# Queries projected ahead of the scores in the first attention rounds, a quarter-size zero buffer, and the delta rule's epsilon scaled by the query's norm

## What is computed

```python
h = layernorm(x) * (1 + ca) + sa
x = x + ga * L0_attn(h)        # layer 0: softmax attention, 16 heads of 8, with a position bias
h = layernorm(x) * (1 + cb) + sb
x = x + gb * L0_ffn(h)         # 8 experts, top 1, capacity 640 each
...
x = x + ga * L1_attn(h)        # layer 1: gated delta rule, 16 value heads, 8 key heads of 64
x = x + gb * L1_ffn(h)         # 16 experts that each pick 512 tokens, and a shared one
```

```python
proj = einsum('bld,ed->ble', x, w_in)          # k, v, q
logits = einsum('bhld,bhmd->bhlm', q, k) * scale + bias
out = einsum('bhlm,bhmd->bhld', softmax(logits), v)
```

```python
q = q * rsqrt(sum(q * q) + EPS) * DK ** (-0.5)
o = ...                                        # linear in q
o = o * rsqrt(mean(o * o) + EPS) * norm_w * silu(z)
```

## Time and profile before

| | |
|---|---|
| median of 3 runs | 2565.08 us (2564.73 to 2572.67) |
| profiled execution | 2562.15 us |
| its span, first to last instruction | 2560.4 us |
| busy: PE, PEld, DVE | 2086.0, 1296.3, 1848.1 us |
| busy: ACT, POOL | 1478.8, 788.8 us |
| granted TensorE clock, mean | 0.896 |
| whole program's DMA | 85.57 MB |

### The profile page before, as it was taken

How to read it: one execution, slowest core, us unless ns; L and a number is a source line. 1 busy time by engine, 2 the same in 40 slices (tenths; PEclk the granted TensorE clock), 3 DMA queues, 4 the chain that set the end, 5 groups by cost and what they waited for, 6 DMA issues and landing times. The chain is left out here.

```text
span 2560.4 us, 64355 instructions
## 1 busy us (share of the span) xinstructions
PE 2086.0 (81%) x25432; PEld 1296.3 (51%) x25432; DVE 1848.1 (72%) x4475; ACT 1478.8 (58%) x4032; POOL 788.8 (31%) x851
## 2 busy tenths in 40 slices
PE   6988988988887585488888888888888884778984
PEld 2444444444444363256655555666555563555552
DVE  6777777777776335799999999899999953673333
ACT  3666766766666124357777777777777663222221
POOL 1000100100100243134444444444444431105884
PEclk7999999999998797689999999999999985788997
DMA  6000000000000431100000000000000003334334
GB/s 231 1 1 5 9 5 5 9 5 5 9 5 5 123 97 41 29 11 13 13 13 13 13 13 13 13 13 13 13 13 5 5 4 104 83 100 105 44 44 89
DMA packets 109980, 85.57 MB, mean 33 GB/s; under 512 B 22430, under 2 KB 97858, under 8 KB 109424
## 3 DMA queue, kind: packets, MB, share of 16 engines
q1 hardware_dynamic: 96112, 68.31, 9.1%
q0 software_dynamic: 13568, 13.14, 3.2%
HBM read 59.22 MB, written 22.71 MB: 32 GB/s over the span
## 5 line engine op out<-in xcount | busy, mean ns | idle before, releaser
L565 ACT ACTIVATE Pr<-Pr,nmax 128x512 f32<-128x512 f32 x512 | 341.2, 715 | 190.2 <-DVE nmax L475 187.7
L706 PE MATMUL bank<-ident,Pr 128*128 128x128 f32 x2048 | 305.6, 292 | 83.1 <-DVE PT L484 62.8
L706 PEld LDWEIGHTS bank<-ident,Pr 128*128 128x128 f32 x2048 | 234.9, 148 | 255.2 <-DVE PT L484 160.5
L475 DVE CUSTOM_DVE_ANT_0 Pr<-bank,Tb 128x512 f32<-128x512 f32 x512 | 330.9, 684 | 29.5 <-PE bank L692 28.8
L484 DVE COPY PT<-bank 128x512 f32<-128x512 f32 x256 | 176.6, 690 | 186.5 <-PE bank L720 182.9
L2469 PE MATMUL bank<-Wcv,hw 128*128 128x512 f32 x512 | 245.8, 624 | 4.9 <-ACT bank L2260 3.4
L2073 DVE TENSOR_TENSOR pr<-AC,Tc 128x30 f32<-128x30 f32 (+14 forms) x480 | 223.7, 466 | 36.0 <-POOL Tc L1946 22.2
L2074 DVE TENSOR_TENSOR Tc<-Tc,pr 128x30 f32<-128x30 f32 (+14 forms) x480 | 189.8, 395 | 16.5
L572 ACT ACTIVATE PT<-bank 128x512 f32<-128x512 f32 x256 | 150.8, 589 | 80.2 <-PE bank L720 74.1
L692 PE MATMUL bank<-kp,qp 8*128 8x512 f32 x1024 | 168.4, 661 | 0.0
L264 POOL DMA_INDIRECT disp<-H,slot x32 | 31.8, 994 | 419.6 <-DVE slot L420 354.1
(11 more groups left out here) (407 smaller groups left out, 4421.7 us busy)
## 6 DMA issues: line engine op xcount, KB each, us to landing
aB<-alpha SPq DMA_DIRECT2D x64, 128.0 KB, 2.8
Tb<-scores SPq DMA_DIRECT2D x4, 1792.0 KB, 13.2
w<-in_L_ffn_W SPq DMA_DIRECT2D x16, 256.0 KB, 5.6
rawW<-in_L_ffn_up_w SPq DMA_DIRECT2D x16, 256.0 KB, 3.2
rawW<-in_L_ffn_gw SPq DMA_DIRECT2D x16, 256.0 KB, 3.9
rawW<-in_L_ffn_down_w SPq DMA_DIRECT2D x16, 256.0 KB, 4.0
disp<-Pr SPq DMA_DIRECT2D x1, 2580.0 KB
xin<-disp SPq DMA_DIRECT2D x8, 322.5 KB, 6.2
```

The lines of the kernel that those rows point to most:

```text
L475: V.tensor_tensor_reduce(out=Pr[:, s, i, :], in0=pS[hh][:, :], in1=Tb[:, h, at:at + L], scale=-1.0, scalar=3.0e38, op0=ALU.add, op1=ALU.mi ...
L565: A_(Pr[:, s, i, :], Pr[:, s, i, :], ACT.Exp, scale=-1.0, bias=nmax[:, s, i:i + 1])\
L706: last = TR(pT[m % 2][:, t * P:(t + 1) * P], Pr[:, (G % 2) * HG + hh, t, j * P:(j + 1) * P], ident[:, :])
```

## The change

Three edits.

1. `first(R)` is the list of the "q" projections of rounds 0, 1 and 2, `rest(R)` all others. TensorE and ScalarE do `first(R)` ahead of the round's scores and exponentials and `rest(R)` where `at_round(R)` was. VectorE's code is the same.
2. `zero` has a quarter of the columns, 1290; the DMA reads it four times for each partition.
3. O's sum of squares is no longer scaled down by the query's squared inverse norm. Instead epsilon is scaled up by the squared norm, once for each pair of chunks (`eq`), and added. Then the root and the reciprocal give the factor for O with no further product. The reciprocal of norms is taken for the keys alone.

```diff
-        zero = part(1, 0, SLOTS0 // P * ROW0)
+        zero = part(1, 0, SLOTS0 // P // 4 * ROW0)
...
+        first = lambda R: [(kind, x) for kind, x in at_round(R) if kind == "q" and 0 <= R < 3]
+        rest = lambda R: [u for u in at_round(R) if u not in first(R)]
...
-                sp.dma_start(g["disp"].rearrange("(p r) d -> p (r d)", p=P), zero).then_inc(r["s_disp"], 16)
+                sp.dma_start(g["disp"].rearrange("(p r q) d -> p r (q d)", p=P, r=4), bcast(zero, 1, 4)).then_inc(r["s_disp"], 16)
...
+                    for kind, x in first(R):
+                        misc(kind, x)
...
-                    for kind, x in at_round(R):
+                    for kind, x in rest(R):
                         misc(kind, x)
...
                 def total(k):
                     dve.wait_ge(s["a_osq"], half(k, 1))
                     n2 = nrm[:, k % 2, :].rearrange("p (k v) -> p k v", v=2)
-                    rq = rkq[:, k // 2 % 3, k % 2, 1, :]
-                    link(V.tensor_tensor(rq2[:, k % 2, :], rq, rq, ALU.mult))
-                    V.tensor_tensor(n2, n2, bcast(rq2[:, k % 2, :], 2, 2), ALU.mult).then_inc(s["v_ss"], 1)
+                    dve.wait_ge(s["v_eq"], k // 2 + 1)
+                    V.tensor_tensor(n2, n2, bcast(eq[:, k // 2 % 3, k % 2, :], 2, 2), ALU.add).then_inc(s["v_ss"], 1)

                 def inverse_norm(k):
                     dve.wait_ge(s["a_or"], k + 1)
-                    n2 = nrm[:, k % 2, :].rearrange("p (k v) -> p k v", v=2)
-                    link(V.reciprocal(nrm[:, k % 2, :], nrm[:, k % 2, :]))
-                    V.tensor_tensor(n2, n2, bcast(rkq[:, k // 2 % 3, k % 2, 1, :], 2, 2), ALU.mult)\
-                        .then_inc(s["v_rn"], 1)
+                    V.reciprocal(nrm[:, k % 2, :], nrm[:, k % 2, :]).then_inc(s["v_rn"], 1)

                 def inverse_norms(m):
                     dve.wait_ge(s["p_nt"], m + 1)
-                    V.reciprocal(rkq[:, m % 3, :, :, :].rearrange("p e w k -> p (e w k)"), BKK[:, 256:256 + 4 * HK])\
-                        .then_inc(s["v_rk"], 1)
+                    n4 = BKK[:, 256:256 + 4 * HK].rearrange("p (e w k) -> p e w k", e=2, w=2)
+                    q2 = eq[:, m % 3, :, :]
+                    link(V.tensor_copy(q2, n4[:, :, 1, :]))
+                    V.reciprocal(rkq[:, m % 3, :, :], n4[:, :, 0, :]).then_inc(s["v_rk"], 1)
+                    V.scalar_tensor_tensor(q2, q2, EPS1 * DK, q2, ALU.mult, ALU.mult).then_inc(s["v_eq"], 1)
...
-                    A_(nrm[:, k % 2, :], nrm[:, k % 2, :], ACT.Sqrt, bias=w["eps"][:, 0:1], scale=1.0 / DK)\
+                    A_(nrm[:, k % 2, :], nrm[:, k % 2, :], ACT.Sqrt, scale=1.0 / DK)\
```

More of the change, by code:

```diff
@@ L1753, in delta1 @@
                     "v_ks", "a_qs", "v_s", "v_o", "v_lt", "v_at", "v_ac", "v_tt", "v_conv", "v_by", "v_ss",
-                    "v_rn", "v_rk", "p_nm", "p_nt", "a_rt", "v_link", "g_x", "g_s", "g_d1", "g_t", "g_t0", "g_halo", "g_on", "g_hw", "g_ac", "v_nm", "a_kq", "g_ud",
+                    "v_rn", "v_eq", "v_rk", "p_nm", "p_nt", "a_rt", "v_link", "g_x", "g_s", "g_d1", "g_t", "g_t0", "g_halo", "g_on", "g_hw", "g_ac", "v_nm", "a_kq", "g_ud",
                     "a_m", "a_w", "a_on", "a_sq", "a_osq", "a_or", "d_al0", "d_al1", "d_out",
@@ L1761, in delta1 @@
         sq = s.sb("sqc", [P, 2, 2, 2, 2, P])
-        rkq = s.sb("rkq", [P, 3, 2, 2, HK])
-        rq2 = s.sb("rq2", [P, 2, HK])
+        rkq = s.sb("rkq", [P, 3, 2, HK])
+        eq = s.sb("eq", [P, 3, 2, HK])
         bk = s.sb("bk", [P, 2, HV])
@@ L1994, in total @@
                     n2 = nrm[:, k % 2, :].rearrange("p (k v) -> p k v", v=2)
-                    rq = rkq[:, k // 2 % 3, k % 2, 1, :]
-                    link(V.tensor_tensor(rq2[:, k % 2, :], rq, rq, ALU.mult))
-                    V.tensor_tensor(n2, n2, bcast(rq2[:, k % 2, :], 2, 2), ALU.mult).then_inc(s["v_ss"], 1)
+                    dve.wait_ge(s["v_eq"], k // 2 + 1)
+                    V.tensor_tensor(n2, n2, bcast(eq[:, k // 2 % 3, k % 2, :], 2, 2), ALU.add).then_inc(s["v_ss"], 1)
                 def inverse_norm(k):
                     dve.wait_ge(s["a_or"], k + 1)
-                    n2 = nrm[:, k % 2, :].rearrange("p (k v) -> p k v", v=2)
-                    link(V.reciprocal(nrm[:, k % 2, :], nrm[:, k % 2, :]))
-                    V.tensor_tensor(n2, n2, bcast(rkq[:, k // 2 % 3, k % 2, 1, :], 2, 2), ALU.mult)\
-                        .then_inc(s["v_rn"], 1)
+                    V.reciprocal(nrm[:, k % 2, :], nrm[:, k % 2, :]).then_inc(s["v_rn"], 1)
                 def inverse_norms(m):
                     dve.wait_ge(s["p_nt"], m + 1)
-                    V.reciprocal(rkq[:, m % 3, :, :, :].rearrange("p e w k -> p (e w k)"), BKK[:, 256:256 + 4 * HK])\
-                        .then_inc(s["v_rk"], 1)
+                    n4 = BKK[:, 256:256 + 4 * HK].rearrange("p (e w k) -> p e w k", e=2, w=2)
[3 more added lines that the diff above has]
+                    V.scalar_tensor_tensor(q2, q2, EPS1 * DK, q2, ALU.mult, ALU.mult).then_inc(s["v_eq"], 1)
                 def norms(m):
                     dve.wait_ge(s["v_rk"], m + 1)
-                    rk = bcast(rkq[:, m % 3, :, 0, :], 3, 2)
+                    rk = bcast(rkq[:, m % 3, :, :], 3, 2)
                     s2, n = m // (NP // 2), 2 * (m % (NP // 2))
```

## The result

| | before | after |
|---|---|---|
| median of 6 runs | 2564.9 us (2558.9 to 2572.67) | 2541.51 us (2535.56 to 2550.71) |
| ratio to before, 95% interval | | 0.993 (0.9904 to 0.9956) |
| profiled execution, its span | 2562.15, 2560.4 us | 2550.71, 2548.9 us |
| start of the last scores that VectorE reads in the attention stage | 820.0 us | 818.2 us |
| delta rule, first to last `read_out` | 1002.8 us | 991.9 us |

Where this text speaks of the gain of the whole program, it goes by the ratio and its interval. The profiled execution happens to be the slowest of its six, so the two traces differ by only 11.4 us, and 10.9 of them lie in the delta rule.

What follows compares the result with a forecast made beforehand. Stages behind barriers add up: TensorE paces setup, a three-engine chain the first attention rounds, VectorE the delta rule, partly held by GpSimd. 0 + 3 - 4 = -1 us, counted from the 2565.08 median: 2564 us, range 2555 to 2571.

Steps and rivals of the forecast that it cites:

- Zero buffer, 0: Setup: memset falls from 4.40 to 1.1 us, but TensorE is never idle between 8 and 20 us, so 0 (-1 to +1).
- Queries ahead, +3: First attention rounds: round 0's scores wait for q1's projection and come 3.0 us late, not won back: +3 us (-3 to +5).
- The ledger, -9.0: Delta rule: instructions removed less those added, 32 x 0.39 - 16 x 0.22 = -9.0 us if VectorE's time were all path.
- A step that reaches a held stretch sooner only waits longer there: Delta rule: VectorE steps held by GpSimd swallow savings made ahead of them; loop taken as -4 us instead of -9.
- Neither GpSimd instruction comes sooner: Delta rule, odd chunk: the GpSimd instructions holding the steps at 1406.53 and 1419.03 follow ScalarE's work and stand still.
- the holds let the saving through: Rival, delta rule: shifted steps start ahead of GpSimd's instruction; loop gives its whole -9, total -6, 2559 us; chance 0.2.
- By that rule carried through, near 0: Delta rule: VectorE and GpSimd excluding each other at SBUF, carried through, leaves the loop's saving near 0 instead of -9 us.
- The rival of the added product held ahead of `read_out`: Delta rule: GpSimd holds the added product about 1.2 us a pair, +18 us; total +12, 2577 us; chance 0.08.
- the signs named for "wrong": Profile: round 3's scores before 57 us, TensorE's clock back before 60, pairs over 0.5 us shorter, new product over 0.3 us.

## Why the prediction was wrong

**Zero buffer, 0: right.** The memset came at 1.18 us instead of the 1.1 taken, the DMA earlier, and TensorE in between did not notice.

**Queries ahead, +3: right, and to 0.2 us in every round** where the clock fell at the same place. Where it falls earlier (the change's own profile) the +3.0 stands too: 37.3 against the 34.3 of the epsilon alone. Whether these 3 us reach the end can't be told: the stage's last scores start anywhere from 810.1 to 825.3 us in the eight traces with the old order, at 818.2, 823.6 and 814.7 in the three with the new, and the queries alone gave a whole time of 1.0009.

**The ledger, -9.0: a little small.** From the start of the reciprocal to that of the instruction behind the pair of them it took 0.38 us (1444.44 in the earlier trace rows, the scan at 1444.82) and takes 0.16 (1435.51 to 1435.67): -0.22, against the estimated 0.20. The square's 0.19 went as counted. The additions put the product `bk` 2.74 us behind the transposition instead of 2.55 (1429.45 to 1432.00 before, 1422.30 to 1425.04 after): +0.19, against 0.22. So a pair has 2 x 0.41 - 0.19 = 0.63 us less of instructions, where I had 0.56: over 16 pairs 10.1, not 9.0. One thing more is missing from both sums: the instruction behind the removed product got shorter too (the scan 1.22 us in before, 1.16 in the change), so that up to the start after it the saving is 0.28 (1444.44 to 1446.07 before, 1435.51 to 1436.86 after) and 0.26 in the odd turn. With that a pair has about 0.73 us less, 11.7 over 16 pairs.

**"A step that reaches a held stretch sooner only waits longer there": this failed.** It is the step that led me from -9 to -4, and the loop measured -12. The page's groups of the substitution steps, after:

```profile
L2078 DVE TENSOR_TENSOR pr<-AC,Tc 128x30 f32<-128x30 f32 (+14 forms) x480 | 206.8, 431 | 33.4 <-POOL Tc L1952 19.6
L2079 DVE TENSOR_TENSOR Tc<-Tc,pr 128x30 f32<-128x30 f32 (+14 forms) x480 | 205.3, 428 | 16.5
```

Their sum is 412.1 us. The same two groups of before:

```profile
L2073 DVE TENSOR_TENSOR pr<-AC,Tc 128x30 f32<-128x30 f32 (+14 forms) x480 | 223.7, 466 | 36.0 <-POOL Tc L1946 22.2
L2074 DVE TENSOR_TENSOR Tc<-Tc,pr 128x30 f32<-128x30 f32 (+14 forms) x480 | 189.8, 395 | 16.5
```

413.5 us. Other steps are held (the second group gained what the first lost), but not for longer: had the holds taken up half of the 10 us saved, the sum would be 5 us larger. It is 410.1 to 413.5 in the three traces without the edit and 409.0 to 412.5 in the six with it. (The idle time before the first step, the wait for GpSimd's `Tc`, tells nothing: 22.2 to 23.6 us without the edit, 19.6 to 23.4 with it.) There are two reasons why the holds took up nothing.

The first is that a premise of that sentence is false: "Neither GpSimd instruction comes sooner". Order of time of one pair, GpSimd, before:

```profile
1366.44 2.51 POOL L1895 TENSOR_TENSOR Xs<-vt,Xs 128x512 f32<-128x512 f32 x2 [7.86 <-DVE Xs L1988]
...
1389.21 2.48 POOL L1923 TENSOR_TENSOR O<-O,zs 128x512 f32<-128x512 f32 x2
...
1401.16 2.50 POOL L1895 TENSOR_TENSOR Xs<-vt,Xs 128x512 f32<-128x512 f32 x2 [8.09 <-DVE Xs L1988]
```

It goes on in the earlier trace rows, at 1406.34, 1418.80 and 1431.57. After:

```profile
1360.35 2.50 POOL L1901 TENSOR_TENSOR Xs<-vt,Xs 128x512 f32<-128x512 f32 x2 [7.72 <-DVE Xs L1994]
...
1382.62 2.49 POOL L1929 TENSOR_TENSOR O<-O,zs 128x512 f32<-128x512 f32 x2
...
1394.59 2.50 POOL L1901 TENSOR_TENSOR Xs<-vt,Xs 128x512 f32<-128x512 f32 x2 [8.08 <-DVE Xs L1994]
...
1400.42 1.06 POOL L1922 TENSOR_TENSOR Ud<-Ws,dl 128x512 f32<-128x512 f32 x1 [1.48 <-ACT Ws L2302]
...
1412.03 1.45 POOL L1929 TENSOR_TENSOR O<-O,zs 128x512 f32<-128x512 f32 x1 [3.59 <-ACT O L2309]
...
1424.61 2.56 POOL L1901 TENSOR_TENSOR Xs<-vt,Xs 128x512 f32<-128x512 f32 x2 [7.72 <-DVE Xs L1994]
```

Counted from the residual (`Xs`) with which each pair starts:

| GpSimd's instruction | before | after | moved |
|---|---|---|---|
| gated O, even turn | 22.77 | 22.27 | -0.50 |
| residual, odd turn | 34.72 | 34.24 | -0.48 |
| weighed `Ud`, odd turn | 39.90 | 40.07 | +0.17 |
| gated O, odd turn | 52.36 | 51.68 | -0.68 |
| residual of the next pair | 65.13 | 64.26 | -0.87 |

By the medians of all common pairs (the three traces without the edit, the six with it) these are -0.47, -0.47, -0.13, -0.60 and -0.85.

The gated O follows ScalarE's scaling of O, and this one moved with it, by the same 0.68 (from 1416.65 to 1409.88 in the two traces, 50.21 and 49.53 after the residual): ScalarE too works on what VectorE gives out. The hold at 1419.03 ends when GpSimd's O ends; that end came sooner, so the held step did.

The second reason is that steps slid past the holder, which is the rival's own mechanism. The weighed `Ud` stood still in this pair, as I had written of both (in other pairs of the same trace it came 0.5 us sooner), and in the change it is the step two places on, at 1400.62, that is held. At the gated O of the odd turn it is one place on:

```profile
1411.98 0.38 DVE L2078 TENSOR_TENSOR pr<-AC,Tc 128x210 f32<-128x210 f32 x1
1412.39 1.32 DVE L2079 TENSOR_TENSOR Tc<-Tc,pr 128x210 f32<-128x210 f32 x1
```

The step that began 0.23 us behind GpSimd's O in before (1419.03) now begins 0.05 ahead of it (1411.98, O at 1412.03), takes 0.38 instead of 1.33, and its successor is held. In 29 of the 30 common pairs without the edit the step held there is this one of 210 columns or one ahead of it; in all 38 with the edit it is a later one. The product out for even k alone does the same with GpSimd's O standing still. The margin of 0.23 was wider than the 0.20 that I had put down as saved, but not wider than the 0.26 really saved ahead of it in that turn.

So a hold passes a saving on when its holder depends, however indirectly, on the engine that is held, and also when the saving is enough for a step to start ahead of the holder. For the first, the sign stood in the brackets of the rows: GpSimd had been idle for 0.8 to 8 us ahead of the residuals, of the `Ud` and of the odd turn's O, waiting for ScalarE or VectorE, and I read that as independence. The even turn's O follows GpSimd's own work without idle time; that work had waited for VectorE's transposition `AC`, at 16.19 us in before and 15.69 in the change, counted as in the table.

The Trainium skill (SBUF — State Buffer, section Who interferes with whom) has the exclusion itself right: of the 85 to 91 substitution steps of each trace that took over 0.9 us, every one ended within 0.3 us after an instruction of GpSimd. "By that rule carried through, near 0" was my step and not the page's; the loop gave -12 us (1000.4 on average in the three kernels without the edit, 988.5 in the six with it).

**The rival "the holds let the saving through", 0.2, was the right one**, by its own mechanism (steps that start ahead of GpSimd's instruction) at the two holds of the odd turn, and because the gated O came sooner in both turns. Its size, -9, falls short by 3, of which the ledger's error is 1.1 by its own way of counting and 2.7 with the shorter instructions behind the products. The rival of the added product held ahead of `read_out` did not occur (113 ns at most). Of the signs named for "wrong", one came: pairs shorter by more than 0.5 us.

**Two kinds of pairs** are a second thing that neither the ledger nor a rival held. Pairs come mostly in two lengths. Order of time of the change, VectorE at the start of a pair of 64.25 us, and of the next one, of 62.66:

```profile
1360.79 0.89 DVE L2024 TENSOR_TENSOR bk<-bT,rkq 128x32 f32<-128x32 f32 x1
1361.60 1.31 DVE L2025 TENSOR_TENSOR gk<-gT,rkq 128x32 f32<-128x32 f32 x1
1362.83 1.93 DVE L2026 COPY rkd<-rkq 128x32 f32<-128x32 f32 x1
...
1425.04 0.88 DVE L2024 TENSOR_TENSOR bk<-bT,rkq 128x32 f32<-128x32 f32 x1
1425.84 0.18 DVE L2025 TENSOR_TENSOR gk<-gT,rkq 128x32 f32<-128x32 f32 x1
1425.95 1.26 DVE L2026 COPY rkd<-rkq 128x32 f32<-128x32 f32 x1
```

GpSimd, behind its two halves of the residual:

```profile
1362.81 1.90 POOL L1913 TENSOR_TENSOR S<-S,GC 128x1024 f32<-128x1024 f32 x1
...
1427.12 1.91 POOL L1913 TENSOR_TENSOR S<-S,GC 128x1024 f32<-128x1024 f32 x1
```

In the long pair `bk` is held to the end of the first half, `gk` (1.31 us) to the end of the second at 1362.8, and the copy `rkd` until GpSimd's decay of S ends at 1364.71. In the short pair `gk` slips in between the halves, for 0.18 us, and `rkd` is held by the second half only: 1.1 us less by then, 1.8 by the first reciprocal of the pair. Both pairs reach `bk` 2.74 us after their transposition, and the residual on GpSimd at 2.30 and 2.31, so what decides lies within about a hundredth of a microsecond. The odds moved all the same: `rkd` starts within 3.7 us of the transposition in 3 of 36 pairs of the three kernels without the epsilon edit (`gk` slipped in between in two of them), and in 20 of 72 with it. Taken apart so, long pairs fell from 65.31 to 64.63 us on average (the common ones among them by 0.85 in the median); short ones are at 62.69 (63.99 in the three without the edit). The mean of all fell by 1.10, which over the 12 pairs counted would be 13.2 us; the loops differ by 11.9, so the pairs left out and the loop's end gave 1.3 back. That the edit itself makes the short pair more frequent is what these counts suggest; no run here puts `gk` there on purpose, and the 20 are 1 to 6 a trace, not independent of each other.

**What stays open.** The prediction's sum with the loop's measured term, 0 + 3 - 12, is -9: 2556 us, just inside the range. So the failed step accounts for 8 of the 17 us (by the ratio) by which the forecast was off, and the rest isn't traced to a place. Either the 3 us of the queries do not reach the end (the queries alone: +3, -4 to +9), or the difference lies in the spread of the whole times. The loops account for 12 us, the whole program's ratios for 13 to 18, with intervals that hold 12 (7 to 19 and, for the first measurement, 11 to 25). In the traces nothing else in the program, from the last scores to the loop and from the loop to the end, showed a difference beyond its scatter from trace to trace.

## What to carry to other kernels

When one engine's steps are held by another's, ask what releases the holder before taking the hold for a fixed wall: if the holder had been idle, waiting for something that follows from the held engine, both move together and a saving goes through. Compare the margin by which a step misses the holder with what is saved ahead of it, counted generously: one step that slips ahead is worth a whole step. A hand-made ledger of starts (each instruction's start to the next one's) gave 0.63 us a pair, 0.73 with the shorter instruction behind, and the common pairs gave 0.85; the correction I put on top of it was the error. And when a projection is put ahead of the scores, move the copies that feed the next projection as well, or the engine only waits at another place.

## What the runs showed of the hardware that I had not expected

- A VectorE instruction on 1024 columns with one input took 3.50 us, to 0.8 us behind the end of the GpSimd memset of 5160 columns that ran beside it, and 0.75 us where the memset (1290 columns) had ended before it began.
- Two small instructions, `gk` and `rkd`, take 3.2 us (1361.60 to 1364.76) or 1.4 (1425.84 to 1427.21) together, by whether the first falls between two instructions of GpSimd or is held by one.
- The same program starts its rounds at 33.3 or 37.3 us in two executions (and the other order at 30.1 or 34.3), by where the granted clock falls to 0.50 ahead of them, about 30 or 25 us. In two traces it fell later still, at 33.2 (zero buffer alone, rounds from 30.3) and at 34.6 (`kp` ahead of the moments, rounds from 32.4 instead of 33.4).
